# Attention on one core: the weigh of a quarter moved behind the turn of the third quarter

## The reference

```python
scores = jnp.einsum('bhqd,bhkd->bhqk', q / math.sqrt(HEAD_DIM), k)
scores = scores + attention_bias            # (2, 16, 2048, 2048), float32
scores = jnp.where(src_mask, -jnp.inf, scores.astype(jnp.float32))
probs = jax.nn.softmax(scores, axis=-1).astype(v.dtype)
ctx = jnp.einsum('bhqk,bhkd->bhqd', probs, v)
```

## Time and profile before

| | us |
|---|---|
| median of 3 runs | 3461.2 (3459.51 to 3461.22) |
| the profiled execution, its own time | 3459.6 |
| its span in the trace | 3457.9 |
| mean granted clock of TensorE | 0.994 of full speed |
| TensorE matmuls busy, of the span | 3401.9 |
| TensorE weight loads busy | 1931.1 |
| VectorE busy | 2473.3 |
| ScalarE busy | 1874.1 |
| GpSimd busy | 2118.7 |

### The profile page before, as it was taken

How to read it: one execution, slowest core, us unless ns; L and a number is a source line. 1 busy time by engine, 2 the same in 40 slices (tenths; PEclk the granted TensorE clock), 3 DMA queues, 4 the chain that set the end, 5 groups by cost and what they waited for, 6 DMA issues and landing times. The chain is left out here.

```text
span 3457.9 us, 60344 instructions
## 1 busy us (share of the span) xinstructions
PE 3401.9 (98%) x18230; PEld 1931.1 (56%) x18230; DVE 2473.3 (72%) x4130; ACT 1874.1 (54%) x2515; POOL 2118.7 (61%) x674
## 2 busy tenths in 40 slices
PE   8999799999999999999999999999899999999998
PEld 3444466666666666666666666666444444444443
DVE  5665599999999999999999999999434334343331
ACT  3222388888888888888888888888111111111010
POOL 0000499999899999899999999998303212221200
PEclk9999899999999999999999999999999999999999
DMA  8999999999999999999999999999823123132000
GB/s 296 342 342 330 380 364 346 346 351 348 397 347 350 350 342 352 399 347 342 353 348 348 392 352 350 349 344 320 234 45 85 43 49 79 42 66 62 12 12 13
DMA packets 243407, 913.81 MB, mean 264 GB/s; under 512 B 27568, under 2 KB 44464, under 8 KB 166064
## 3 DMA queue, kind: packets, MB, share of 16 engines
q1 hardware_dynamic: 177920, 810.38, 65.5%
q10 hardware_dynamic: 62896, 94.65, 7.9%
q0 software_dynamic: 2560, 8.39, 0.7%
HBM read 770.46 MB, written 142.87 MB: 264 GB/s over the span
## 5 line engine op out<-in xcount | busy, mean ns | idle before, releaser
L675 POOL TENSOR_TENSOR ring<-ring,penb 128x1856 f32<-128x1856 f32 x511 | 1898.4, 3760 | 129.3 <-DMA ring<-in_fside_Bx16xSxS 87.3
L784 ACT ACTIVATE ring<-ring,low 128x2048 f32<-128x2048 f32 x512 | 1029.1, 2010 | 299.6 <-DVE low L752 299.5
L866 PEld LDWEIGHTS b_T<-ident,ring 128*128 128x128 f32 x8192 | 890.3, 141 | 430.5 <-DVE probT L736 428.2
L866 PE MATMUL b_T<-ident,ring 128*128 128x128 f32 x8192 | 1091.7, 276 | 3.3 <-DVE probT L736 3.3
L752 DVE CUSTOM_DVE_ANT_0 ring<-scores,ring 128x1024 f32<-128x1024 f32 x512 | 627.1, 1225 | 173.4 <-PE scores L832 157.0
L736 DVE COPY probT<-b_T 128x512 f32<-128x512 f32 x1024 | 702.9, 687 | 4.2 <-PE b_T L866 4.1
L752 DVE CUSTOM_DVE_ANT_0 ring<-scores,ring,low_part 128x1024 f32<-128x1024 f32 x512 | 653.0, 1275 | 1.2 <-issue 0.5
L832 PE MATMUL scores<-keys,queries 128*128 (+1 forms) x2048 | 621.7, 425 | 15.3 <-ACT ring L784 11.9
L889 PE MATMUL bank_ctx<-probT,values 128*32 128x512 f32 x4096 | 545.3, 605 | 0.0
L796 ACT COPY probT<-b_T 128x512 f32<-128x512 f32 x1024 | 538.7, 576 | 2.8 <-PE b_T L866 2.7
L1218 ACT ACTIVATE keys_again<-scores,b_scaled 128x512 f32<-128x512 f32 x128 | 88.0, 687 | 732.5 <-PE scores L1442 732.5
(11 more groups left out here) (134 smaller groups left out, 2068.5 us busy)
## 6 DMA issues: line engine op xcount, KB each, us to landing
ring<-in_fside_Bx16xSxS SPq DMA_DIRECT2D x512, 1024.0 KB, 7.5
keys<-k_rows SPq DMA_DIRECT2D x64, 1024.0 KB, 8.4
queries<-q_rows SPq DMA_DIRECT2D x128, 256.0 KB, 8.0
values<-v_heads ACTq DMA_DIRECT2D x128, 256.0 KB, 6.4
ctx_scratch<-ctxp ACTq DMA_DIRECT2D x128, 256.0 KB, 6.3
penb<-ctx_scratch SPq DMA_DIRECT2D x120, 256.0 KB, 10.3
k_rows<-part_hi SPq DMA_DIRECT2D x64, 256.0 KB, 3.1
k_rows<-part_lo SPq DMA_DIRECT2D x64, 256.0 KB, 3.1
```

The costliest lines, as they stand in the source:

```text
L675: nc.gpsimd.tensor_tensor(ring[:, j, 0:POOL_MASKED], ring[:, j, 0:POOL_MASKED], penb[:, j, 0:POOL_MASKED], ALU.add).then_inc(masked, 1)
L784: nc.scalar.activation(ring[:, k, :], ring[:, k, :], ACT.Exp, bias=low[:, k:k + 1], scale=-1.0, accum_out=column(sums_all, trip, k)).then_ ...
L866: last = nc.tensor.transpose(turn_bank(slot, n)[:, c * P:(c + 1) * P], ring[:, slot, at:at + P], ident[:])
```

## The change

TensorE's step now turns quarters 0, 1 and 2, then weighs, then turns quarter 3. The wait for ScalarE's copy of quarter 0 goes from the middle of quarter 2 to the head of quarter 3, and `copied_before_weigh` from the middle of quarter 1 to the middle of quarter 2. The wait at the head of quarter 2 (L855) stays at the head of quarter 2. No other engine's program changes.

```diff
@@ -853,14 +853,14 @@
             t, slot = it * R + j - 2, (j - 2) % R
             if n == 2 and live(t, NT):
                 need(pe, out_dve, t * 2)
+            if n == 3 and live(t, NT):
+                pe.wait_ge(out_act, t * 2 + 1)
             for c in range(QR):
                 if c == 2:
                     if n == 0 and live(t, NT):
                         need(pe, out_act, t * 2)
-                    if n == 1:
+                    if n == 2:
                         copied_before_weigh(it, j)
-                    if n == 2 and live(t, NT):
-                        pe.wait_ge(out_act, t * 2 + 1)
                 if live(t, NT):
                     at = (QR * n + c) * P
                     last = nc.tensor.transpose(turn_bank(slot, n)[:, c * P:(c + 1) * P], ring[:, slot, at:at + P], ident[:])
@@ -896,8 +896,8 @@
             score(it, j, 1)
             turn(it, j, 0)
             turn(it, j, 1)
+            turn(it, j, 2)
             weigh(it, j)
-            turn(it, j, 2)
             turn(it, j, 3)
 
         trips(pe, step, after)
```

## The result

The changed kernel takes 3898.1 us, median of three runs (3897.4 to 3907.1), against 3461.2 before: 12.7% slower, ratio 1.1268 with a 95% interval of 1.1253 to 1.1282. The profiled execution took 3898.07 us, 438.5 more than the profiled one of before (3459.6). The forecast was 3910, in a range of 3865 to 3945.

A forecast was written before the change was run, and what follows sets the result against it. TensorE's order of work was taken as the bound; the bared wait at quarter 2 makes steps 2.86 + 0.59 + 1.00 + 0.39 = 4.84 us against 3.95, so 506 x 0.89 = 450 on 3459.6 gives 3910, range 3865 to 3945.

The forecast's parts named there:

- What bounds: Attention steps: TensorE's order of work sets the 3.95 us step, VectorE close behind with 3.64 us of work.
- The hole: Head of quarter 2 (L855): TensorE stops from about 2.0 us of the step until its load at 2.86.
- the steps without a weigh: First steps of attention, quarters in the change's order: held load starts 0.05 us after VectorE's copy ends.
- The bare hole: TensorE between quarters 1 and 2: still for about 0.85 us a step, so the step is 82% busy or a little over.
- What follows it: After quarter 2's load: 0.59 us to the weigh, 1.00 for the weigh, 0.39 for quarter 3; step 4.84 us.
- The sum: Attention: 506 steps x 0.89 us = 450 us on top of 3459.6, so 3910.
- half of the weigh's entry: Entry into the weigh behind quarter 2: losing half of it takes 45 us off, at the range's lower end.
- The other waits: L863's wait at quarter 3 and `copied_before_weigh` in quarter 2 cost nothing; ScalarE's copy has 1.4 us slack at group ends.
- The clock: TensorE in attention: granted clock stays 1.00; rival, 3 in 100: falls to 1.2 GHz in the holes, 5460 us.
- Slower, but by less: Weigh behind held quarter 2: its entry costs nothing, -0.20 us a step, 3809 us; 5 in 100.
- Faster: Scores' last load: its 0.18 us hold by quarter 2's copy goes, 91 us less, 3369; 1 in 100.

The follow-up runs named there:

- The dose: VectorE fill of 128 columns added between the first add and the copy of quarter 3: 3483.1 us in the kernel before, 3938.4 in the changed one.
- the version with the weigh last: Changed kernel with the weigh behind quarter 3 as well, after all four quarters: 3958.9 us.
- the chain-cut version: Changed kernel with VectorE copying quarter 3 before its first add instead of behind it: 3445.0 us, ratio to before 0.995.
- the two chain-cut kernels: VectorE's copy of quarter 3 moved before its first add: 3445.7 us in the kernel before, 3445.0 in the changed kernel.

## Why the prediction was right

- **What bounds.** Right: TensorE's order of work, with the copy's release 0.25 us inside the weigh. The dose in the kernel before, in which the held load still came 0.32 us behind the copy's end (1503.73 to 1504.05), and the renamed idle time show it.
- **The hole.** Quarter 2 was put at 2.86 us of the step; it comes at 1508.96 - 1506.10 = 2.86. The 0.05 us from the copy's end, taken from the steps without a weigh, is found again here and in the versions with the dose (1507.29 to 1507.34) and with the weigh last. In all 373 steps of the changed kernel from 500 to 2300 us the held matmul starts 0.06 us behind the copy's end. The bare hole of about 0.85 us was counted from the end of quarter 1; the matmuls' recorded idle time is 0.69, so they are busy for 86% of the stretch and not 82%. The sum uses neither.
- **What follows it.** 0.59, 1.00 and 0.39 were used; the rows give 0.59 (1508.96 to 1509.55), 1.00 (to 1510.55) and 0.38. So 4.83 instead of 4.84.
- **The sum.** 12 us too high. A step was to grow by 4.84 - 3.95 = 0.89 us; it grew by 4.827 - 3.952 = 0.875. Over 506 steps the new step is 6.6 of the 12 us and the old one 1.0, and the stages behind attention took 3.2 us less. In the range, half of the weigh's entry of 0.20 us is 506 x 0.10 = 51 us and not 45, so its lower end should be 3859; the result lies well inside either way.
- **The other waits.** ScalarE's copy at quarter 3 has 1.4 us of slack as worked out, and the version with the weigh last shows the price without cover. The moved wait of L863 costs nothing (ratio 1.0003), and neither does `copied_before_weigh`, since the chain-cut version has it in the new place and shows no loss.
- **The clock.** It stayed at 1.00, at 86% busy matmuls with a hole of 0.69 us in each step. The rule of the Trainium skill on transposes ("TensorE: Matmul & The Clock Gate", Part 4: PE-mode transpose) spoke for a fall, and none came. Since 13 of the 29 matmuls of a step are no transposes, this does not show whether a transpose counts for the clock.
- **The rivals.** "Slower, but by less" is out: the load of the weigh comes 0.59 behind quarter 2's, its entry of 0.20 us included. "Faster" named the hold of the scores' last load. That hold is gone from the changed kernel (1.5 us in all instead of 74.2), but what it was worth is far less than the new hole: the chain-cut version, also without it, gains 16 us on the kernel before, not the 91 of the rival.
- **Not foreseen:** that ScalarE's copies are a second chain of the same kind, which holds TensorE by 0.26 us a step when the weigh is put ahead of quarter 0. This does not touch the forecast; the 3460 us expected of that version looked at VectorE alone.

## What to carry to other kernels

When a piece of work is moved on a busy engine, write down for each wait behind it when its releaser is done, counted from the start of the step, and compare that with when the engine would arrive there without the piece. If the releaser needs this step's own first result, the wait closes a loop and its bare part is paid in every step. Then look at the releasing engine's order too: moving one copy ahead of one `add` made both places of the weigh cost the same and beat both kernels (3445.0 us), for no instruction more. It did not free every place: ahead of quarter 0 the weigh still cost 42 us more.

## What the runs showed that was not expected

- The idle time of weight loads ahead of transposes, 0.84 us a step behind a weigh, appears with three different releasers, and with each of them the matmuls went on. The idle time of the *matmuls* in the same rows is the one that counts.
- A wait that is met late near the end of a loop's body made the loop's jump visible: 0.48 us a trip, where the two chain-cut kernels with the weigh behind quarter 1 or 2 show none. That the late wait is the cause is read from the traces, not tested.
- A short VectorE instruction between two others cost 0.08 us, half of its record of 0.17.
